# Second-layer attention of a two-layer transformer kernel: a new order of the work within a batch, two projections in halves, the normalisation spread over four steps, and the output store issued by another queue

## The reference

```
xn = layernorm(x)                                  # 8 batches, 512 tokens, 256 features
q, k, v = split(xn @ Wqkv.T); 16 heads of 16
logits = q @ k.T / 4 + pos_bias[head, i - j]       # 512 x 512 for each of 8 x 16 heads
attn = softmax(logits)                             # with its row maximum taken out first
out = (attn @ v) @ Wout.T                          # the attention's output, 8 x 512 x 256
```

## Time and profile before

| | us |
|---|---|
| median of 3 runs | 2039.24 (2036.27 to 2040.58) |
| profiled execution, device time | 2048.42 |
| its span, first to last instruction | 2046.7 |
| the changed stage, first score to last output copy | 1194.4 to 1855.8 |
| mean granted TensorE clock over the span, of 2.4 GHz | 0.93 |

### The profile page before, as it was taken

One profiled execution on the slowest core, in us unless ns is written; L12 is line 12 of the kernel. 1 busy time (PEld: TensorE's weight loads), 2 busy tenths in 40 slices (PEclk: granted clock), 3 DMA queues, 4 the chain that ended last, 5 costly groups with the idle time before them and its releaser, 6 DMA issues. The chain is left out here.

```text
span 2046.7 us, 34076 instructions
## 1 busy us (share of the span) xinstructions
PE 1773.9 (87%) x11015; PEld 1149.2 (56%) x11015; DVE 1150.4 (56%) x2519; ACT 1066.1 (52%) x1455; POOL 978.8 (48%) x736
## 2 busy tenths in 40 slices
PE   4988988887999999999996967878878778877999
PEld 3455555544788888888885733333334333326566
DVE  5666566662253353443433368767877877845435
ACT  2455555555532232232322228877877878885642
POOL 2344444432344444434432528766766767784202
PEclk7899999997999999999998959989889888988999
DMA  3333333324420121111201442222122222116456
GB/s 120 86 104 101 90 93 89 93 66 148 160 80 24 56 68 35 56 54 38 67 27 55 160 151 78 82 60 79 56 76 90 62 68 77 42 55 228 129 157 209
DMA packets 119261, 182.74 MB, mean 89 GB/s; under 512 B 14197, under 2 KB 73077, under 8 KB 119162
## 3 DMA queue, kind: packets, MB, share of 16 engines
q1 hardware_dynamic: 110076, 171.11, 27.4%
q10 hardware_dynamic: 8448, 8.39, 1.2%
q0 software_dynamic: 640, 2.10, 0.3%
HBM read 90.72 MB, written 39.91 MB: 64 GB/s over the span
## 5 line engine op out<-in xcount | busy, mean ns | idle before, releaser
L835 POOL TENSOR_TENSOR l_prob<-l_prob,l_bias 128x1024 f32<-128x1024 f32 x192 | 452.8, 2378 | 165.0 <-ACT l_prob L991 164.3
L1268 POOL TENSOR_TENSOR f_hl<-f_full,f_hh 128x512 fp32r<-128x512 f32 x192 | 248.4, 1294 | 410.3 <-DVE f_hh L1306 270.5
L1049 DVE CUSTOM_DVE_ANT_0 l_slot<-l_slot,l_bias 128x512 f32<-128x512 f32 x512 | 340.5, 715 | 73.0 <-PE l_slot L1128 62.9
L994 ACT ACTIVATE l_prob<-l_prob 128x1024 f32<-128x1024 f32 x256 | 270.9, 1070 | 0.0
L493 DVE TENSOR_REDUCE l_peak<-l_slot 128x2 f32<-128x256 f32 (+3 forms) x256 | 206.3, 822 | 108.8 <-PE l_slot L585 105.6
L1356 PE MATMUL f_ps<-f_hh,f_hi_h 128*128 128x512 f32 x1024 | 260.3, 390 | 3.4 <-ACT f_hh L1280 2.5
L1356 PE MATMUL f_ps<-f_hl,f_hi_h 128*128 128x512 f32 x1024 | 258.3, 389 | 0.0
L397 ACT ACTIVATE l_prob<-l_slot 128x1024 f32<-128x1024 f32 (+3 forms) x256 | 175.4, 706 | 100.8 <-PE l_slot L604 97.9
L991 ACT COPY l_prob<-l_slot 128x1024 f32<-128x1024 f32 x192 | 194.7, 1014 | 50.1 <-PE l_slot L1144 49.5
L1356 PEld LDWEIGHTS f_ps<-f_hh,f_hi_h 128*128 128x128 f32 x1024 | 192.0, 188 | 46.7 <-issue 3.2
L1356 PEld LDWEIGHTS f_ps<-f_hl,f_hi_h 128*128 128x128 f32 x1024 | 192.2, 188 | 39.9
(11 more groups left out here) (228 smaller groups left out, 2811.7 us busy)
## 6 DMA issues: line engine op xcount, KB each, us to landing
l_stacks<-l_parts SPq DMA_DIRECT2D x384, 128.0 KB, 2.6
attn<-l_out_sb ACTq DMA_DIRECT2D x16, 512.0 KB, 3.1
f_raw<-in_L_ffn_h_w SPq DMA_DIRECT2D x16, 512.0 KB, 4.1
f_raw<-in_L_ffn_h_w SPq DMA_DIRECT2D x32, 256.0 KB, 2.6
e_w<-in_L_ffn_f SPq DMA_DIRECT2D x32, 256.0 KB, 3.0
l_bias<-ext SPq DMA_DIRECT2D x16, 448.0 KB, 8.5
l_x_in<-in_L_attn_x SPq DMA_DIRECT2D x8, 512.0 KB, 3.9
xh<-l_xh SPq DMA_DIRECT2D x8, 512.0 KB, 2.6
```

Of the source, the lines that this page charges most:

```text
L835: return eng.tensor_tensor(probs(n), src, bias[:, h:h + 2, j * P:j * P + T], ALU.add)
L994: act.activation(probs(n), probs(n), ACT.Exp).then_inc(p_exp.sem, 1)
L1049: ins = dve.tensor_tensor_reduce(src, src, bias[:, 4 * g + 2 * pr + a, t * P:t * P + T], 1.0, 3 * NEG, ALU.add, ALU.max, peak[:, g, a, pr, ...
L1268: pool.tensor_tensor(t.hl[layer % 2][:, o], t.full[:, n % 2], t.hh[layer % 2][:, o].bitcast(F32), ALU.subtract).then_inc(self.h_lo.sem, 1)
```

## The change

It alters only where pieces stand, into which banks they go, and who issues one DMA; the arithmetic is the same.

- `v` and `out` are each computed in two halves of 12 matmuls with a copy each. The halves of `v` stand in steps 17 and 18 and share one pair, which stays out of the rotation for that time (`PLACE` skips one place after score 17). The halves of `out` stand in steps 30 and 31 and use `single`.
- `ln` is one tile a step (steps 11 to 14), with the shift of its own at step 10 and `ln_rstd` at step 7.
- `qk` 0 and 1 go to steps 21 and 26; `qk` 2 and 3 go out of the preparation and into the batch's own turn, steps 5 and 7. DVE's low part (`qk_low`) stands behind the step's score. `stack`, `mix_turn`, `heads_turn` move with them; the first group's `heads_turn` goes from step 26 to step 0 of the next turn.
- The store is SP's event at step 31 instead of ACT's.

```diff
-        off, s = later((27, 28, 36, 44)[g] - STEPS)
+        off, s = later((29, 30, 41, 44)[g] - STEPS)
         placed[s].append(("stack", off, g))
-    for g, s in enumerate((26, 34, 42, 52)):
+    for g, s in enumerate((32, 35, 43, 52)):
         off, s = later(s)
         placed[s] += [("heads_turn", off, g), ("heads_norm", off, g)]
-    for s, *events in ((0, ("x_load", 1, 0)), (17, ("v", 0, 0)),
+    for s, *events in ((0, ("x_load", 1, 0)), (17, ("v", 0, 0)), (18, ("v", 0, 1)),
                        (3, ("ln_stats", 1, 0)), (4, ("ln_stats", 1, 1)), (5, ("ln_stats", 1, 2)),
-                       (6, ("ln_stats", 1, 3), ("ln_rstd", 1, 0)), (8, ("ln", 1, 0)),
-                       (18, ("x_turn", 1, 0)), (19, ("x_turn", 1, 1)), (22, ("qk", 1, 0)), (23, ("qk", 1, 1)),
-                       (24, ("mix_turn", -1, 0)), (27, ("mix_turn", -1, 1)), (28, ("qk", 1, 2)), (29, ("qk", 1, 3)),
-                       (31, ("out", -1, 0), ("store", -1, 0))):
+                       (6, ("ln_stats", 1, 3)), (7, ("ln_rstd", 1, 0)), (10, ("ln_shift", 1, 0)),
+                       (11, ("ln", 1, 0)), (12, ("ln", 1, 1)), (13, ("ln", 1, 2)), (14, ("ln", 1, 3)),
+                       (18, ("x_turn", 1, 0)), (19, ("x_turn", 1, 1)), (21, ("qk", 1, 0)), (26, ("qk", 1, 1)),
+                       (5, ("qk", 0, 2)), (7, ("qk", 0, 3)), (23, ("mix_turn", -1, 0)), (28, ("mix_turn", -1, 1)),
+                       (30, ("out", -1, 0)), (31, ("out", -1, 1), ("store", -1, 0))):
         placed[s] += events
     for s in range(STEPS):
         STEADY += placed[s]
+        lows = [("qk_low", off, n) for kind, off, n in placed[s] if kind == "qk"]
         STEADY.append(("prob", 0 if s >= LAG else -1, (s - LAG) % STEPS))
...
         STEADY.append(("score", 0, s))
+        STEADY += lows
...
-    PAIRED = [e for e in STEADY if e[0] in ("score", "prob", "v", "out")]
-    SINGLE = [e for e in STEADY if e[0] in ("maxima", "x_turn", "qk", "heads_turn", "mix_turn")]
-    assert len(PAIRED) % 3 == 0
+    PAIRED = [e for e in STEADY if e[0] in ("score", "prob") or e[0] == "v" and e[2] == 0]
+    PLACE, turn_of = {}, 0
+    for kind, off, n in PAIRED:
+        PLACE[kind, n], turn_of = turn_of, (turn_of + 1) % 3
+        if (kind, n) == ("score", 17):
+            turn_of = (turn_of + 1) % 3
+    SINGLE = [e for e in STEADY if e[0] in ("maxima", "x_turn", "qk", "heads_turn", "mix_turn", "out")]
+    assert turn_of == 0
...
+                if kind == "store":
+                    wait(sp, out_ready, TT // 2, b)
+                    sp.dma_start(out_d[b].rearrange("(t p) d -> p t d", p=P), out_sb[:]).then_inc(out_saved.sem, 16)
...
                 if kind == "ln" and not opening(b):
-                    wait(act, xn_saved, 1, b - 1)
-                    wait(act, shift_ready, 1, b)
-                    for t in range(TT):
-                        act.activation(xn[:, t], x_in[:, t], ACT.Identity, bias=shift[:, t:t + 1],
-                                       scale=rstd[:, t:t + 1]).then_inc(xn_ready.sem, 1)
+                    if n == 0:
+                        wait(act, xn_saved, 1, b - 1)
+                        wait(act, shift_ready, 1, b)
+                    act.activation(xn[:, n], x_in[:, n], ACT.Identity, bias=shift[:, n:n + 1],
+                                   scale=rstd[:, n:n + 1]).then_inc(xn_ready.sem, 1)
...
                 if kind == "out":
-                    wait(act, out_saved, 1, b - 1)
-                    wait(act, out_ps, 1, b)
-                    act.copy(out_sb[:].rearrange("p (a t) d -> p a (t d)", a=2), slot(kind, 0)[:])\
+                    if n == 0:
+                        wait(act, out_saved, 1, b - 1)
+                    wait(act, out_ps, n + 1, b)
+                    act.copy(out_sb[:, 2 * n:2 * n + 2].rearrange("p t d -> p (t d)"), single[:])\
                        .then_inc(out_ready.sem, 1)
-                if kind == "store":
-                    wait(act, out_ready, 1, b)
-                    act.dma_start(out_d[b].rearrange("(t p) d -> p t d", p=P), out_sb[:]).then_inc(out_saved.sem, 16)
...
-                if kind == "qk":
+                if kind == "qk_low":
                     wait(dve, high_ready, n + 1, b)
...
                     if n == 0 and opening(b):
-                        wait(pe, low_ready, 4, b)
+                        wait(pe, low_ready, 2, b)
```

More of the change, by code:

```diff
@@ L776, in released @@
             return (p_copied, added(k)[1]) if pooled(k) else added(k)
-        return LAST_READ[kind], k + 1
+        return LAST_READ[kind], 2 if kind == "v" else k + 1
     def slot(kind, n):
-        return slots[[(u[0], u[2]) for u in PAIRED].index((kind, n)) % 3]
+        return slots[PLACE[kind, n]]
     def bank(kind, n, b):
-        if not opening(b):
+        if not opening(b) or n >= 2:
             return single[:]
-        return slots[2][:, n] if kind == "x_turn" else slots[n // 2][:, n % 2]
+        return slots[2 if kind == "x_turn" else 0][:, n]
     def there(b):
@@ L979, in emit @@
                 if kind == "v":
-                    wait(act, v_ps, 1, b)
+                    wait(act, v_ps, n + 1, b)
                     if opening(b):
@@ L983, in emit @@
                     wait(act, value_ps, QUADS * TT, b - 1)
-                    act.copy(vals[:, :, 0:HD], slot(kind, 0)[:].rearrange("p a (n d) -> p (a n) d", d=HD))\
-                       .then_inc(v_ready.sem, 1)
+                    half = vals[:, TT // 2 * H * n:TT // 2 * H * (n + 1), 0:HD]
+                    act.copy(half, slot(kind, 0)[:, n].rearrange("p (n d) -> p n d", d=HD)).then_inc(v_ready.sem, 1)
                 if kind == "prob":
@@ L1072, in _, with claim @@
         def _(pe):
-            def claim(uses, depth, kind, n, i):
+            def claim(uses, same, kind, n, i):
                 at = [(u[0], u[2]) for u in uses].index((kind, n))
-                for m in range(at - depth, at - len(uses) - 1, -depth):
+                for m in range(at - 1, at - len(uses) - 1, -1):
                     before, off, k = uses[m]
+                    if not same(before, k):
+                        continue
                     bb = i + off - (1 if m < 0 else 0)
@@ L1111, in emit @@
                         pe.wait_ge(w_ready.sem, 3)
-                    out = claim_pair(kind, n, i)
-                    for t in range(TT):
-                        ins = product(out[:, t // 2, (t % 2) * D:(t % 2 + 1) * D],
+                    out = claim_pair(kind, 0, i) if n == 0 else slot(kind, 0)
+                    for t in range(2 * n, 2 * n + 2):
+                        ins = product(out[:, n, (t % 2) * D:(t % 2 + 1) * D],
                                       [((xl if q else xh)[:, k, t * P:(t + 1) * P], wv[:, p, k])
@@ L1151, in emit @@
                     if n == 0:
-                        wait(pe, v_ready, 1, b)
+                        wait(pe, v_ready, 2, b)
                         if opening(b):
@@ L1177, in emit @@
                         pe.wait_ge(w_ready.sem, 4)
-                    out = claim_pair(kind, n, i)
+                    claim_single(kind, n, i)
                     wait(pe, ml_ready, KD, b)
-                    for t in range(TT):
-                        ins = product(out[:, t // 2, (t % 2) * D:(t % 2 + 1) * D],
+                    for t in range(2 * n, 2 * n + 2):
+                        ins = product(single[:, (t % 2) * D:(t % 2 + 1) * D],
                                       [(mixt[:, q, k, t * P:(t + 1) * P], wo[:, p, k]) for k in range(KD)
```

26 lines of the change are left out of this document (14 added, 12 removed).

## The result

The changed kernel takes 2026.58 us (median of 5 runs, 2023.62 to 2028.34), the kernel before in the same rounds 2039.24 (2034.96 to 2045.96): ratio 0.9928, 95% interval 0.9899 to 0.9956. It is faster, but by 12.7 us and not by the 35.4 of the forecast. The profiled execution is 2023.62, span 2022.0, mean clock 0.942. The spans of the two profiled executions differ by 24.7; 5.4 of it lie ahead of the first score (1194.4 to 1189.0), where nothing was changed. The profiled one of before was 9.2 over its median and this one is 3.0 under its own, so differences of the two traces show where time went, and the medians how much.

What follows compares the result with a forecast made beforehand. Waits among engines loaded to three quarters, tied by three PSUM pairs, set the turn. Gains of 6.0 us in six turns (36.0), plus 1.0 and 3.4, minus 5.0, gave 35.4 less: 2004 us, range 1990 to 2016 (eight in ten: 1985 to 2034).

Steps and rivals of the forecast that it cites:

- the 3.0 of the jump: DVE's idle 3.01 us at score 0 of a looped turn, taken as a jump cost no edit touches.
- a loss of 1.9: Steps 0 to 7: added q and k pieces and head turn cost 1.9 us a turn, bounds 0 and 4.
- steps 30 and 31: Output projection in halves lets a prob and a score pass between: 2.6 us a turn gained, bounds 1.0 and 3.2.
- DVE has score 0 to do in that time: Steps 0 to 7: PE is held behind the maxima's transpose, but DVE has score 0 to work on meanwhile.
- Steps 8 to 16: Normalisation: shift's wait of 1.61 and part of the tile block go, 2.2 us a turn gained, bounds 0 and 3.8.
- Steps 17 to 20: Halved v lets two score and prob pairs in between: 0.8 us a turn gained, bounds 1 lost and 1.5 gained.
- Steps 21 to 29: Two q and k pieces and a head turn leave: 2.3 us a turn gained, bounds 0.5 and 4.3.
- The end: Next stage's loads queue behind the store on SP: 5.0 us lost, bounds 2 and 8; PE starts 5.5 behind.
- A: Rival: waits come back a step later, 2.3 us a turn gained, 2028 us in all; chance 0.18.
- D: Rival: spread blocks lower PE's clock below about 0.83 in the turn, slower, 2059 us; chance 0.10 including greater end loss.
- C: Rival: steps 0 to 7 take the other stretches' gains, within 0.2% of 2039; chance 0.05; sign: they exceed 23 us.

Runs made afterwards that it cites:

- e4: Changed kernel with turns 1 to 6 written out instead of looped, no jump: 1991.53 us, ratio 0.9751.
- e5: Kernel before the change with its looped turns 1 to 6 written out: 2022.51 us, ratio 0.9913.
- e8: Changed kernel with the x load moved behind DVE's jump and each store cut to one row; only stop and turns read: stop 3.5 to 3.7 us.
- e15: Kernel before the change, looped, with 48 idle semaphore counts on DVE ahead of the stage's first turn: 2029.76 us, ratio 0.9937.
- e13: Changed kernel, looped, with 48 idle semaphore counts on DVE ahead of the stage's first turn: 1995.87 us, ratio 0.9779.
- e1: Changed kernel with the first head group's turn moved from step 0 to step 2 of the next turn: 2027.48 us, ratio 0.9938.
- e2: Changed kernel with the first head group's turn at step 27 of its own turn, ahead of the jump: 2033.49 us, ratio 0.9943.
- e11: Changed kernel with turns written out, all four normalisation tiles back in step 11 and both halves of v in step 17: 2017.14 us, ratio 0.9882.
- e12: Changed kernel with two turns in each loop pass, leaving two jumps back of five: 2008.98 us, ratio 0.9844.
- e3: Changed kernel with the store back in ACT's queue instead of SP's: 2033.38 us, ratio 0.9961.

## Why the prediction was wrong

The direction was right, the size was not, and the failed step is one: "DVE has 13.83 and the 3.0 of the jump", and "I take a loss of 1.9, the added DVE work and nothing for disorder". I read DVE's idle 3.01 us as a fixed cost "which no edit touches". The jump measured 6.4 us in these steps of the changed kernel and 3.1 in the one before (e4, e5), so the stretch lost 5.3 us, outside its bounds of 0 and 4, while the added work cost 2.0 as forecast. The stop is DVE fetching instructions at the jump, a cost that hangs on where the body stands and on what the other pieces do around it. Three things make the 3.3 between the two kernels, each about 1:

- *The stop is longer*, 4.9 against 3.5 us. Without the store's data it is 3.5 (e8), and the stretch about 1 shorter in three of five turns.
- *Less of it is hidden.* Before, PE gave score 0 only at 1502.27, behind the output projection, 0.6 us after DVE had run dry, and with its two matmuls 1.1 of DVE's stop lay beside work that wasn't ready. The halved projection is done earlier, and now all 4.23 us are bare. The stall that I counted as gained in steps 30 and 31 had been the cover of this one. That is 1.1 by the rows; no run takes it alone, but with the stop gone (e15) DVE does wait 1.34 us for that score.
- *PE stands behind it.* I wrote that PE would be held behind the transpose "but DVE has score 0 to do in that time". DVE had nothing to do in that time: the jump comes before the head turn's reader. The pieces in the single bank then restart one behind the other, at half clock: PE is busy 17.00 us in this stretch and 14.70 in e13, for one matmul fewer. e1 and e2 measured about 1 for the place of the head turn; what the clock makes of the 3.3 no run takes alone.

The other steps:

- Steps 8 to 16, 2.2 forecast, 2.2 measured, by another way: the shift's wait of 1.5 stayed, only the block behind it went (2.0 in e11). That the number fits is luck.
- Steps 17 to 20, 0.8 forecast, 0.1 measured. Putting the halves of v back into one step costs 1.6 (e11), yet the stretch gained next to nothing on the kernel before, with PE busy 10.21 against 10.23; why stays open.
- Steps 21 to 29 and 30, 31: 2.3 and 2.6 forecast, 3.4 and 2.9 measured, within the bounds.
- The end: 5.0 forecast, 4.3 measured; PE starts 7.4 us behind the store, where 5.5 was named.
- A's 2028 was near, but not its mechanism: the waits on scores and on the output did go. D did not come: the clock was 0.86 in steps 0 to 7 and 0.91 in steps 8 to 16, 1.00 in the other three stretches, and in steps 0 to 7 it was 1.00 once the stop was gone (e13). The "wrong" sign that I had named for C, steps 0 to 7 over 23 us, is the one that came.

The sum of the work itself stood up: with the jump cheap in both kernels, in the same rounds, they take 2029.76 and 1995.87 us, 33.9 apart, where 35.4 was forecast; written out (e5, e4) they are 31.0 apart. The change lost most of the 21 us between that and 12.7 to the jump that it did not touch: the 48 counts gain 13.6 us in the kernel before (2043.37 to 2029.76) and 30.7 in the changed one (2026.58 to 1995.87, in different rounds); the other 4 are the kernel before's own two medians, 2039.24 and 2043.37.

## What to carry to other kernels

An idle time on "issue" at a loop's head is a cost with a cause, not a constant. Ask whether the body fits, try a shift of a few dozen instructions or write the turns out, before judging any change to the order. And when a stall goes, look for another that had lain under it: here the projection's wait had covered a third of the jump's stop.

## What was new about the hardware

- DVE's jump at the loop's end took 0.30 us or 3.5 to 6.8 us with the same body of 268 or 270 recorded instructions, by where the body stood in the engine's program; shifts of 48 and 560 instructions cured it, 256 did not. PE's body in the same loop, 478 records without its matmuls, jumped in 0.27 to 0.29.
- The fetch can be seen: five instruction packets of 8 KB for each dear jump, none at a cheap one. In e12, with a body of 530, further ones come behind 148, 276 and 403 records of the body, one for each 127 or 128.
- The Trainium skill, Advanced Engine Details and Errata, section Control Flow Timing, gives about 108 ns for a compare-and-branch; here the jump's own record lasts 0.06 us on DVE, and the 0.30 us at best run to the sequencer's next record, so the two are not the same measure.
- The dear jump depends on other queues: in the changed order it was 3.5 us with the store's data left out, 4.9 with the store on SP, 5.3 to 6.8 with it on ACT, yet 3.5 to 4.0 in the kernel before, which also stores from ACT. Moving the x load, of the same size as the store, behind the jump took off 0.1 to 0.3 only. What varies is when the second instruction packet starts: 1.1 to 1.3 us behind the jump in e8, 1.6 to 2.1 before, 2.9 to 3.0 after, 3.3 to 4.9 in e3; DVE goes on 1.8 to 1.9 us later in all but e8 (2.2 to 2.5). Why the store holds that packet up so, and the load does not, stays open.
